# A block of two feed-forward layers around an attention layer: rows of the later feed-forward norms turned by VectorE and DRAM instead of TensorE

## Chip, cores and metric

The kernel runs on one core of one Trainium2 chip. The metric is the device time of one execution in microseconds (us); the time of a run of the kernel before is the median of three, 376.88 us.

## The reference

The input has 16 sequences of 256 rows with 128 features. All is float32; the weights of the feed-forward layer are -1, 0 or 1 with a scale per output column.

```
x = x + 0.5 * ffn(layernorm(x))
x = x + attention(layernorm(x))          # (with a second norm inside, gamma and beta)
x = x + 0.5 * ffn(layernorm(x))

ffn(x):  h = silu(x W1 s1) * (x W2 s2);  h = gelu(h H1 sh1);  h = gelu(h H2 sh2);  return h W3 s3
attention(x):  h = LN(x) gamma + beta;  keys = h Wk + bk;  values = h Wv + bv
               w = exp((keys Wka + bka) / sqrt(128));  w = w / cumsum(w)
               return cumsum(w * keys) * values
```

The hidden width is 512. Both feed-forward layers use the same weights. Cumulative sums run along a sequence.

## The kernel before

The 4096 rows are cut into 8 tiles of 512. Each tile goes through the feed-forward layer, the attention layer and the feed-forward layer again, so there are 16 feed-forward tiles (t = 0 to 15; t from 8 on is the second pass) and 8 attention tiles. Everything stays in SBUF. The residual lies transposed, features on the partitions, in `xt_sb`; matmuls take and give this layout. A norm needs rows on the partitions: for t < 8 they come from `x_sb`, else TensorE turns a tile of `xt_sb` into the bank `y_ps` (stage `u`, four transposes of 128x128, L462).

A norm has these stages. VectorE takes `stats` (four `bn_stats`, L825), `aggr` (a `memset` of one column and four `bn_aggr`, L827 to L832) and `veps` (two small instructions, L839 and L840). GpSimd raises to the power -0.5 and multiplies (`norm`, L362 and L364). ScalarE writes the normalised rows to `z` (stage `z`, four instructions, L726; `zwait` is its wait). TensorE turns `z` into the bank `xt_ps` (stage `t`, `transpose4`, L462). For a feed-forward tile ScalarE copies the bank to `xn_hi`, rounded to fp32r (L764), and VectorE writes the rest to `xn_lo` (L913); for an attention tile ScalarE writes `h_t` with gamma and beta (L767).

The feed-forward layer runs in fp32r with each activation split into a high and a low part, so that two matmuls of 512 columns stand for one product (L449). Stage `p1` gives `gate_ps` and `up_ps` from `xn_hi` and `xn_lo` (four chunks of four matmuls), `p2` and `p3` the hidden layers in `hid_ps` (four chunks of eight each), and `p4` gives `y_ps` (eight). ScalarE does `tanh`, `gelu2`, `gelu3` and the high parts (`high1` to `high3`), VectorE does `gate`, `up`, the low parts (`low1` to `low3`, L877) and the residual (`dt`, L930). The attention has three fp32 products (`att_logits`, `att_keys`, `att_values`; L632, L629, L635), an exponential on ScalarE, which loads its table there and back, and on VectorE two scans, two reciprocals (L940) and some products.

There is no planner at run time. `START`, `SECOND_LAYER`, `FIRST_STEP`, `ORDER` and `LAST_STEP` are lists written out, one per engine and step, and `schedule` issues each engine's stages in that order; semaphores couple the engines. A step i is about one feed-forward tile of PE's time. `AHEAD` says how many tiles a stage runs ahead of the step: `stats`, `z` and `u` two, `t`, `p1`, `tanh`, `gate`, `up` one. The middle repeats a group of three steps with two attention tiles (`a` and `b`) four times. The buffer `z` is single: ScalarE writes the next `z` when TensorE has turned the last one (`s_t`). SyncE (SP) only issues the loads, and at the end seven stores of 256 KB and two halves of the last (L340, L343).

Of the kernel before, what the change touches and what calls it, by code (L numbers as in the profile page):

```python
# [4 lines left out]
P = 128  # L5
# [8 lines left out]
TOK = 512  # L14
# [18 lines left out]
        "hi:w1 hi:w2 zwait z",  # L33
        "t vec:s1 bits:h1.1 bits:h1.3 tanh.0 tanh.1 tanh.2 high1.0 tanh.3 high1.1 zwait z.0 z.1 high1.2 bits:h2.0 "
# [15 lines left out]
FIRST_STEP = {  # L50
# [6 lines left out]
}  # L57
ORDER = {
# [5 lines left out]
    ),  # L64
    "ACT": (
# [24 lines left out]
LAST_STEP = {  # L90
    "PE": "p2.0 p2.1 p2.2 p2.3 p4 p3.0 p3.1 p3.2 last:p4a last:p3.0 last:p3.1 last:p4b last:p4c.0 last:p4c.1",
    "ACT": "gelu2.0 gelu2.1 high2.0 high2.1 gelu2.2 high2.2 gelu2.3 high2.3 gelu3.0 high3.0 gelu3.1 high3.1 "
           "gelu3.2 high3.2 last:gelu.0 last:gelu.1",
    "DVE": "low2.0 low2.1 low2.2 low2.3 low3.0 low3.1 dt low3.2 last:dt.0 last:dt.1",
}

POOL_FIRST = ("norm", 1, 2)

AHEAD = {"stats": 2, "aggr": 2, "veps": 2, "norm": 2, "zwait": 2, "z": 2, "t": 1, "p1": 1, "tanh": 1, "gate": 1,
         "up": 1, "high1": 1, "low1": 1, "u": 2, "p4": -1, "dt": -1}  # L100


def macaron_block(nc, x, xt, w1t, w2t, h1t, h2t, w3t, wkt, wkat, wvt, wkn, vecs, out, seq):
# [8 lines left out]
    GROUP, ATT = 3, 2
    FIRST = 2
    LOOPS = NT // ATT
    assert FIRST + GROUP * LOOPS + 2 == 2 * NT
# [883 lines left out]
```

## Time and profile before

| | |
|---|---|
| median of 3 runs | 376.88 us (376.24 to 377.13) |
| span of the profiled execution, first to last instruction | 374.9 us |
| own time of that execution | not recorded; the median lies 1.98 us above the span |
| TensorE busy | 368.0 us |
| VectorE busy | 321.9 us |
| ScalarE busy | 314.1 us |
| GpSimd busy | 52.6 us |

The profile shows one execution. Busy time is the time in which an engine has an instruction under way; instructions of one engine overlap at their ends, so the distance from one start to the next (the pitch) can be shorter than the duration. TensorE's granted clock is full in every slice of the page. A chain of work is followed back from the last instruction: at each step to what released it, or to the instruction before it on its engine.

### The profile page before, as it was taken

Reading aid. Unit: us, or ns where it says so; the run is one execution under the profiler, and the core shown is the slowest. Engines: PE = TensorE matmul, PEld = TensorE weight load, DVE = VectorE, ACT = ScalarE, POOL = GpSimd, SP = SyncE. Lnnn points to the kernel's source line nnn. Section 1 sums busy time; section 2 is a strip of 40 time slices with the busy share of each in tenths; the row PEclk is TensorE's granted clock in tenths of the full one; section 3 lists DMA queues with packets and bytes.
Section 4 is the critical chain, followed back from the end, with each engine's and each line's share of the span. In section 5 each row is a group of like instructions: output and inputs, shape, how many; then the busy total and the mean of one; then the engine's idle time right before and its main releaser. Section 6 shows DMA issues by size and latency. Waiting matters only on the chain.

```text
span 374.9 us, 5278 instructions
## 1 busy us (share of the span) xinstructions
PE 368.0 (98%) x1662; PEld 291.9 (78%) x1662; DVE 321.9 (86%) x713; ACT 314.1 (84%) x549; POOL 52.6 (14%) x67
## 2 busy tenths in 40 slices
PE   7999999999999999999999999999999999999996
PEld 2678888787787877778788787778877778788885
DVE  5898787999999799999988999989799999976733
ACT  4999699989977999798699979967998998686763
POOL 3531101202101202201021120102101210020000
PEclk9999999999999999999999999999999999999999
DMA  7760000000000000000000000000000000000001
GB/s 246 277 265 1 2 0 0 1 2 1 0 2 0 1 2 2 2 0 1 2 0 1 2 1 28 2 28 1 2 29 0 0 30 1 30 1 28 2 0 58
DMA packets 4494, 9.81 MB, mean 26 GB/s; under 512 B 625, under 2 KB 1905, under 8 KB 4209
## 3 DMA queue, kind: packets, MB, share of 16 engines
q1 hardware_dynamic: 3744, 8.65, 6.3%
q10 hardware_dynamic: 720, 0.80, 0.6%
q8 instruction: 15, 0.25, 0.2%
q14 instruction: 15, 0.11, 0.1%
HBM read 7.35 MB, written 2.10 MB: 25 GB/s over the span
## 4 chain that ended last, share of the span: by engine, by line
PE 95%; DMA 2%; DVE 1%; SPq 1%; issue 0%; ACT 0%; ACTq 0%
PE hid_ps L449 60%; PE gate_ps L449 8%; PE y_ps L449 7%; PE up_ps L449 7%; PE xt_ps L462 3%; DMA x_sb<-x 2%; PE y_ps L462 2%; PE xt_ps L632 2%; PE xt_ps L629 2%; PE xt_ps L635 2%; PE up_ps L507 1%; PE gate_ps L507 1%; DVE gate L855 0%; PE xt_ps L449 0%; DVE xt_sb L924 0%
## 5 line engine op out<-in xcount | busy, mean ns | idle before, releaser
L449 PE MATMUL hid_ps<-act_hi,hi_h 128*128 128x512 f32 x480 | 195.6, 408 | 0.0
L449 PE MATMUL hid_ps<-act_lo,hi_h 128*128 128x512 f32 x480 | 186.8, 389 | 0.0
L877 DVE TENSOR_TENSOR act_lo<-full,act_hi 128x512 fp32r<-128x512 f32 x185 | 122.2, 683 | 26.8 <-ACT act_hi L708 24.3
L701 ACT ACTIVATE full<-hid_ps,vec 128x512 f32<-128x512 f32 x123 | 84.4, 686 | 34.9 <-PE hid_ps L449 31.2
L449 PEld LDWEIGHTS hid_ps<-act_hi,hi_h 128*128 128x128 f32 x480 | 90.1, 188 | 22.4 <-issue 4.1
L449 PEld LDWEIGHTS hid_ps<-act_lo,hi_h 128*128 128x128 f32 x480 | 90.2, 188 | 22.1 <-issue 4.3
L708 ACT ACTIVATE act_hi<-full 128x512 fp32r<-128x512 f32 x127 | 78.5, 630 | 2.3
L362 POOL TENSOR_TENSOR rstd<-veps,half 128x4 f32<-128x4 f32 x24 | 35.2, 1467 | 272.5 <-DVE veps L840 272.5
L855 DVE SCALAR_TENSOR_TENSOR gate<-tanh,gate_ps 128x512 f32<-128x512 f32 x60 | 40.6, 679 | 9.2 <-ACT tanh L684 8.6
L684 ACT ACTIVATE tanh<-gate_ps,s_half 128x512 f32<-128x512 f32 x60 | 40.8, 686 | 8.2 <-PE gate_ps L449 8.2
L867 DVE SCALAR_TENSOR_TENSOR full<-up_ps,s_half,gate 128x512 f32<-128x512 f32 x60 | 44.2, 742 | 0.9
L689 ACT ACTIVATE act_hi<-full 128x512 fp32r<-128x512 f32 x60 | 37.3, 621 | 0.2
L940 DVE RECIPROCAL rcsum<-csum 128x256 f32<-128x256 f32 x16 | 27.9, 1743 | 0.0
L449 PE MATMUL gate_ps<-xn_hi,hi_w 128*128 128x512 f32 x59 | 24.7, 419 | 0.0
L726 ACT ACTIVATE z<-y_ps,nmr,rstd 128x128 f32<-128x128 f32 x64 | 24.0, 460 | 0.8 <-POOL nmr L364 0.8
L449 PE MATMUL y_ps<-act_hi,hi_w 128*128 128x512 f32 x60 | 24.2, 403 | 0.0
L449 PE MATMUL y_ps<-act_lo,hi_w 128*128 128x512 f32 x60 | 23.5, 392 | 0.0
L449 PE MATMUL gate_ps<-xn_lo,hi_w 128*128 128x512 f32 x59 | 23.0, 390 | 0.0
L449 PE MATMUL up_ps<-xn_lo,hi_w 128*128 128x512 f32 x59 | 23.0, 390 | 0.0
L449 PE MATMUL up_ps<-xn_hi,hi_w 128*128 128x512 f32 x59 | 23.0, 390 | 0.0
L825 DVE BATCH_NORM_STATS2 stats<-y_ps 128x6 f32<-128x128 f32 x64 | 14.2, 285 | 0.0
L462 PE MATMUL xt_ps<-ident,z 128*128 128x128 f32 x90 | 13.6, 273 | 0.0
(159 smaller groups left out, 397.8 us busy)
## 6 DMA issues: line engine op xcount, KB each, us to landing
xt_sb<-xt SPq DMA_DIRECT2D x1, 2048.0 KB, 10.9
out<-xt_sb SPq DMA_DIRECT2D x7, 256.0 KB, 2.0
x_sb<-x SPq DMA_DIRECT2D x1, 1536.0 KB, 6.6
raw_h<-h2t SPq DMA_DIRECT2D x4, 256.0 KB, 7.3
raw_h<-h1t SPq DMA_DIRECT2D x2, 256.0 KB, 5.9
raw_w<-w2t ACTq DMA_DIRECT2D x1, 256.0 KB, 4.0
raw_w<-w1t SPq DMA_DIRECT2D x1, 256.0 KB, 3.8
raw_h<-h1t ACTq DMA_DIRECT2D x1, 256.0 KB, 6.7
```

Source lines behind the costliest of these rows:

```text
L362: eng.tensor_tensor(rstd[:, :], veps[:, :], half[:, :], ALU.pow).then_inc(s_pow, 1)
L449: mm = eng.matmul(ps, w, a, start=(first and n == 0), stop=(last and n == len(seq_) - 1))
L462: mm = eng.transpose(dst[:, j * P:(j + 1) * P], src[:, j * P:(j + 1) * P], ident[:, :])
L684: eng.activation(tanh_b[m % 2][:, :], gate_home(T, m)[:, :], ACT.Tanh, scale=s1_half[:, m:m + 1]).then_inc(s_tanh, 1)
L689: eng.activation(act_hi[first_act(T)][:, m, :], full1[m % 2][:, :], ACT.Copy).then_inc(s_hi[1], 1)
L701: eng.activation(full23[m % 2][:, :], home23(n, T, m)[:, :], ACT.Gelu, scale=col("sh1" if n == 2 else "sh2", m)).then_inc(s_gelu[n], 1)
L708: eng.activation(act_hi[n][:, m, :], full23[m % 2][:, :], ACT.Copy).then_inc(s_hi[n], 1)
L726: zz = eng.activation(z[:, j * P:(j + 1) * P], norm_blk(kind, t, j), ACT.Identity, bias=nmr[:, j:j + 1], scale=rstd[:, j:j + 1])
L855: eng.scalar_tensor_tensor(gate_b[m % 2][:, :], tanh_b[m % 2][:, :], 1.0, gate_home(T, m)[:, :], ALU.add, ALU.mult).then_inc(s_gate, 1)
L867: eng.scalar_tensor_tensor(full1[m % 2][:, :], up_home(T, m)[:, :], s12_half[:, m:m + 1], gate_b[m % 2][:, :], ALU.mult, ALU.mult).then_in ...
L877: eng.tensor_tensor(act_lo[a][:, m, :], full[m % 2][:, :], act_hi[a][:, m, :].bitcast(F32), ALU.subtract).then_inc(s_lo[n], 1)
L940: eng.reciprocal(rcsum[:, b], csum[:, b]).then_inc(s_rc, 1)
```

## The change

Three things are changed, and the orders of all engines with them.

First, the rows of the feed-forward norms of tiles 3 to 15 (all but `BY_PE`) are not turned by TensorE. VectorE transposes `z` in blocks of 32x32 into `zt_b` (stage `turn`), SyncE writes that to the DRAM scratch `turns` and, when it has landed, reads it back in four transfers with the blocks in their places (pieces of 32 elements) into `xnt_b`. ScalarE's and VectorE's stage `t` read `xnt_b` from SBUF instead of `xt_ps`. Both buffers are double. The next `z` waits for `s_turn`. The attention's norms and the tiles 0 to 2 are still turned by TensorE.

Second, from norm 3 on the statistics of the halves are pooled on GpSimd (`aggregate`, seven small instructions) instead of `bn_aggr` and `veps` on VectorE. `stats` has two buffers.

Third, the orders are one list of 16 steps for each engine (`STEPS`), SyncE and GpSimd among them. The attention tiles a0 to a7 are spread over steps 1 to 13. `zwait` is part of `z`.

```diff
...
-        "p2.0 a:u t p2.1 p2.2 p1.0 p1.1 p2.3 p1.2 a:t p4 p1.3 a:logits u p3.0 p3.1 a:keys p3.2 p3.3",
...
-        "a:stats low2.0 a:aggr t a:veps low2.1 gate.0 up.0 gate.1 up.1 low2.2 gate.2 low1.0 low2.3 dt up.2 low1.1 "
-        "stats gate.3 aggr up.3 veps a:cumsum low3.0 a:recip.0 low1.2 low3.1 low1.3 low3.2 a:recip.1 low3.3",
...
+STEPS = {
...
+        "a0:norm norm",
...
+        "p2.0 p4 p2.1 u p1.0 p1.1 p2.2 p2.3 p1.2 a4:u a3:values p3.0 p3.1 p1.3 p3.2 p3.3",
...
+        "gelu2.0 t high2.0 tanh.0 tanh.1 gelu2.1 high2.1 z gelu2.2 high2.2 gelu2.3 high2.3 high1.0 gelu3.0 "
+        "tanh.2 high1.1 high3.0 tanh.3 gelu3.1 high3.1 high1.2 9:t high1.3 gelu3.2 a4:z gelu3.3 high3.2",
...
+        "gate.0 5:low3.2 up.0 5:low3.3 a2:weight_keys a2:pool low2.0 a2:values low2.1 a2:dt gate.1 up.1 "
+        "low1.0 dt low2.2 low2.3 stats gate.2 low1.1 gate.3 up.2 up.3 a3:cumsum turn low3.0 a3:recip.0 low3.1 "
+        "low1.2 low1.3 low3.2 low3.3",
+        "a3:recip.1 dt t stats low2.0 a3:weight gate.0 gate.1 a3:weight_keys up.0 up.1 turn low2.1 a4:stats "
+        "low2.2 low2.3 a3:pool low1.0 gate.2 low1.1 up.2 low3.0 gate.3 up.3 9:t low3.1 low1.2 low1.3 "
+        "a3:values a3:dt low3.2",
...
+BY_PE = (0, 1, 2)
+AGGREGATE = 3
...
+        zt_b = [sb(f"zt_{i}", [P, TOK]) for i in range(2)]
+        xnt_b = [sb(f"xnt_{i}", [P, TOK]) for i in range(2)]
+        turns = nc.dram_tensor("turns", [2, P, TOK], F32).ap()
...
+        by_dma = [key for key in norm_of if key[0] == "ffn" and key[1] not in BY_PE]
+        pe_turns = [sum(1 for k, m in norm_of.items() if m <= n and k not in by_dma) for n in range(3 * NT)]
+        dma_turns = [sum(1 for k, m in norm_of.items() if m <= n and k in by_dma) for n in range(3 * NT)]
+        turn_of = {key: k for k, key in enumerate(by_dma)}
+
+        def slot(kind, t):
+            k = turn_of[kind, t]
+            return k % 2, k // 2
...
-            for t in range(NT - 1):
-                eng.wait_ge(s_x1, NT + t + 1)
-                eng.dma_start(out[:, t * TOK:(t + 1) * TOK], xt_tile(t)).then_inc(s_out, 16)
+            def turn(kind, t):
+                i, use = slot(kind, t)
+                eng.wait_ge(s_turn, turn_of[kind, t] + 1)
+                if use > 0:
+                    eng.wait_ge(s_turned[i], 64 * use)
+                eng.dma_start(turns[i], zt_b[i][:, :]).then_inc(s_parked[i], 16)
+                if use > 0:
+                    before, at = by_dma[turn_of[kind, t] - 2]
+                    eng.wait_ge(*((s_xlo, at) if before == "ffn" else (s_ht, at + 1)))
+                eng.wait_ge(s_parked[i], 16 * (use + 1))
+                blocks = turns[i].rearrange("(s c) (j q r) -> q c j s r", c=32, j=SUB, r=32)
+                for b in range(4):
+                    eng.dma_start(xnt_b[i][32 * b:32 * b + 32, :].rearrange("c (j s r) -> c j s r", j=SUB, r=32),
+                                  blocks[b]).then_inc(s_turned[i], 16)
+
+            def emit(stage, chunk, t):
+                if stage in ("turn", "att_turn"):
+                    turn("ffn" if stage == "turn" else "att", t)
+                elif stage == "store":
+                    eng.wait_ge(s_x1, t + 1)
+                    eng.dma_start(out[:, (t - NT) * TOK:(t - NT + 1) * TOK], xt_tile(t)).then_inc(s_out, 16)
+
+            schedule("SP", emit, "rest")
...
+            def aggregate(n):
+                stats, done = stats_b[n % 2], 6 * (n - AGGREGATE)
+                a, b = (1.0 + EPS, EPS * EPS) if n in att_norms else (1.0, EPS)
+                eng.wait_ge(s_bn, SUB * n + SUB)
+                eng.tensor_tensor(pair_diff[:, :], stats[:, :, 1], stats[:, :, 4], ALU.subtract).then_inc(s_agg, 1)
+                eng.tensor_tensor(pair_sum[:, :, :], stats[:, :, 1:3], stats[:, :, 4:6], ALU.add).then_inc(s_agg, 1)
+                eng.wait_ge(s_agg, done + 1)
+                eng.tensor_tensor(diff_sq[:, :], pair_diff[:, :], pair_diff[:, :], ALU.mult).then_inc(s_agg, 1)
+                eng.wait_ge(s_agg, done + 2)
+                eng.tensor_scalar(var_part[:, :], pair_sum[:, :, 1], a / P, b, ALU.mult, ALU.add).then_inc(s_agg, 1)
+                eng.wait_ge(s_agg, done + 3)
+                eng.tensor_scalar(diff_part[:, :], diff_sq[:, :], a / 4.0, None, ALU.mult).then_inc(s_agg, 1)
+                eng.tensor_scalar(neg_mean[:, :], pair_sum[:, :, 0], -0.5, None, ALU.mult).then_inc(s_agg, 1)
+                eng.wait_ge(s_agg, done + 5)
+                eng.tensor_tensor(veps[:, :], var_part[:, :], diff_part[:, :], ALU.add).then_inc(s_ve, 1)
+                eng.wait_ge(s_agg, done + 6)
+
             def norm(n):
-
+                if n >= AGGREGATE:
+                    aggregate(n)
...
+                n = norm_of[kind, t]
+                first = SUB - act_z(n)
+                if not pair:
+                    eng.wait_ge(s_nmr, n + 1)
+                    if n > 0:
+                        eng.wait_ge(s_t, pe_turns[n - 1])
+                    if n > 0 and dma_turns[n - 1]:
+                        eng.wait_ge(s_turn, dma_turns[n - 1])
...
+                elif stage == "t" and t not in BY_PE:
+                    i, use = slot("ffn", t)
+                    eng.wait_ge(s_p1, MC * t)
+                    eng.wait_ge(s_turned[i], 64 * (use + 1))
+                    eng.activation(xn_hi[:, :], xnt_b[i][:, :], ACT.Copy).then_inc(s_xhi, 1)
...
+                if n >= 2:
+                    eng.wait_ge(s_nmr, n - 1)
                 for j in range(SUB):
                     if (n, j) == (0, SUB // 2):
                         eng.wait_ge(s_x0_half, 16)
-                    eng.bn_stats(stats[:, j, :], norm_blk(kind, t, j)).then_inc(s_bn, 1)
+                    eng.bn_stats(stats_b[n % 2][:, j, :], norm_blk(kind, t, j)).then_inc(s_bn, 1)
...
+                elif stage in ("turn", "att_turn"):
+                    kind = "ffn" if stage == "turn" else "att"
+                    i, use = slot(kind, t)
+                    eng.wait_ge(s_za, norm_of[kind, t] + 2)
+                    if use > 0:
+                        eng.wait_ge(s_parked[i], 16 * use)
+                    eng.transpose(zt_b[i][:, :], z[:, :]).then_inc(s_turn, 1)
...
+                elif stage == "t" and t not in BY_PE:
+                    i, _ = slot("ffn", t)
+                    eng.wait_ge(s_xhi, t)
+                    eng.tensor_tensor(xn_lo[:, :], xnt_b[i][:, :], xn_hi[:, :].bitcast(F32),
+                                      ALU.subtract).then_inc(s_xlo, 1)
```

(The longest lists are left out; of `STEPS`, step 7 of PE, ACT and DVE stands.) What the prediction uses of the other steps: in step 6 DVE has `... gate.3 up.2 up.3 a3:cumsum turn low3.0 a3:recip.0 low3.1 low1.2 low1.3 low3.2 low3.3` before step 7's `a3:recip.1 dt t`, and PE `... p1.3 u a3:logits p3.0 p3.1 a3:keys p3.2 p3.3`. For tile 15, step 13 has `... low3.0 turn low1.2 low3.1 ...` on DVE and `... p3.0 p3.1 p3.2 p3.3` on PE, step 14 `gelu2.0 high2.0 gelu2.1 high2.1 gelu2.2 t ...` on ACT (for tile 15) and `p2.0 p2.1 p2.2 p2.3 p4 p1.0 ...` on PE.

## Rows read from the trace of the kernel before

**Rows 1.** The page: span, busy time by engine, and VectorE's busy tenths in 40 slices.

```profile
span 374.9 us, 5278 instructions
...
PE 368.0 (98%) x1662; PEld 291.9 (78%) x1662; DVE 321.9 (86%) x713; ACT 314.1 (84%) x549; POOL 52.6 (14%) x67
...
DVE  5898787999999799999988999989799999976733
```

**Rows 2.** The page: the chain that ended last, shares of the span.

```profile
PE 95%; DMA 2%; DVE 1%; SPq 1%; issue 0%; ACT 0%; ACTq 0%
```

**Rows 3.** Stretches: length, busy time by engine (instructions), clock, DMA share, GB/s.

```profile
26.00:372.00 346.00, 345.65 (x1563) 277.62 (x1562) 300.82 (x648) 294.27 (x509) 41.04 (x44) 1.00 0.02 6
138.00:208.00 70.00, 70.00 (x318) 55.77 (x317) 64.65 (x143) 61.32 (x106) 9.48 (x10) 1.00 0.00 1
```

**Rows 4.** The chain in order of time: start us, length us, what.

```profile
119.31 5.44 PE hid_ps L449 x24
124.75 0.44 PE y_ps L462 x4
125.19 0.44 PE xt_ps L462 x4
...
236.73 7.30 PE hid_ps L449 x32
...
306.61 7.30 PE hid_ps L449 x32
```

**Rows 5.** Groups of instructions: count, busy us, mean ns, idle before.

```profile
L940 DVE RECIPROCAL rcsum<-csum 128x256 f32<-128x256 f32 x16 | 27.9, 1743 | 0.0
...
L462 PE MATMUL xt_ps<-ident,z 128*128 128x128 f32 x90 | 13.6, 273 | 0.0
```

**Rows 6.** Timeline of VectorE: start us, us, line, operation, count.

```profile
144.43 2.43 DVE L877 TENSOR_TENSOR act_lo<-full,act_hi 128x512 fp32r<-128x512 f32 x4
...
149.51 0.89 DVE L825 BATCH_NORM_STATS2 stats<-y_ps 128x6 f32<-128x128 f32 x4
...
164.83 0.18 DVE L832 BATCH_NORM_AGGREGATE mv<-stats 128x2 f32<-128x6 f32 x1
...
165.12 1.24 DVE L935 TENSOR_TENSOR_SCAN csum<-ones,kw 128x256 f32<-128x256 f32 x2
...
189.78 0.16 DVE L839 TENSOR_SCALAR neg_mean<-mv 128x4 f32<-128x4 f32 x1
...
189.92 0.69 DVE L877 TENSOR_TENSOR act_lo<-full,act_hi 128x512 fp32r<-128x512 f32 x1
190.74 0.75 DVE L867 SCALAR_TENSOR_TENSOR full<-up_ps,s_half,gate 128x512 f32<-128x512 f32 x1
```

**Rows 7.** Timeline of GpSimd.

```profile
152.09 2.52 POOL L362 TENSOR_TENSOR rstd<-veps,half 128x4 f32<-128x4 f32 x1 [9.18 <-DVE veps L840]
...
190.09 1.38 POOL L362 TENSOR_TENSOR rstd<-veps,half 128x4 f32<-128x4 f32 x1 [19.88 <-DVE veps L840]
...
198.33 1.01 POOL L362 TENSOR_TENSOR rstd<-veps,half 128x4 f32<-128x4 f32 x1 [6.18 <-DVE veps L840]
199.41 0.20 POOL L364 TENSOR_TENSOR nmr<-neg_mean,rstd 128x4 f32<-128x4 f32 x1
```

**Rows 8.** Timeline of ScalarE; in brackets the idle time before it.

```profile
154.92 1.51 ACT L726 ACTIVATE z<-y_ps,nmr,rstd 128x128 f32<-128x128 f32 x4 [0.38 <-POOL nmr L364]
```

**Rows 9.** Transfers: SyncE's issues, queue 1, and issues by size with us to landing.

```profile
13.79 0.43 SPq L335 DMA_DIRECT2D wk<-wkt  x1
...
14.74 0.65 SPq L335 DMA_DIRECT2D wv<-wvt  x1
...
q1 hardware_dynamic: 3744, 8.65, 6.3%
...
out<-xt_sb SPq DMA_DIRECT2D x7, 256.0 KB, 2.0
...
wk<-wkt SPq DMA_DIRECT2D x1, 64.0 KB, 6.1
```

More of the change, by code:

```diff
@@ L49 @@
 )
-FIRST_STEP = {
[6 rows of a table removed]
-}
-ORDER = {
[5 rows of a table removed]
+STEPS = {
+    "SP": (
+        "",
+        "turn",
+        "turn",
+        "turn",
+        "turn",
+        "turn",
+        "turn",
+        "turn",
+        "turn",
+        "store turn",
+        "store turn",
+        "store turn",
+        "store turn",
+        "store turn",
+        "store",
+        "store",
+    ),
+    "POOL": (
+        "norm",
+        "norm",
+        "a0:norm norm",
+        "a1:norm norm",
+        "norm",
+        "a2:norm norm",
+        "a3:norm norm",
+        "norm",
+        "a4:norm norm",
+        "a5:norm norm",
+        "norm",
+        "a6:norm norm",
+        "a7:norm norm",
+        "norm",
+        "",
+        "",
+    ),
[19 rows of a table added]
     ),
     "ACT": (
[10 rows of a table removed]
[42 rows of a table added]
     ),
     "DVE": (
-        "a:stats low2.0 a:aggr t a:veps low2.1 gate.0 up.0 gate.1 up.1 low2.2 gate.2 low1.0 low2.3 dt up.2 low1.1 "
-        "stats gate.3 aggr up.3 veps a:cumsum low3.0 a:recip.0 low1.2 low3.1 low1.3 low3.2 a:recip.1 low3.3",
-        "b:stats a:weight b:aggr t b:veps a:weight_keys low2.0 a:pool gate.0 a:values gate.1 low2.1 a:dt up.0 up.1 "
[6 rows of a table removed]
-    ),
-}
[L90 to L95, printed above, removed]
[39 rows of a table added]
+    ),
+}
 POOL_FIRST = ("norm", 1, 2)
-AHEAD = {"stats": 2, "aggr": 2, "veps": 2, "norm": 2, "zwait": 2, "z": 2, "t": 1, "p1": 1, "tanh": 1, "gate": 1,
-         "up": 1, "high1": 1, "low1": 1, "u": 2, "p4": -1, "dt": -1}
+BY_PE = (0, 1, 2)
+AGGREGATE = 3
+AHEAD = {"stats": 2, "aggr": 2, "veps": 2, "norm": 2, "z": 2, "t": 1, "p1": 1, "tanh": 1, "gate": 1,
+         "up": 1, "high1": 1, "low1": 1, "u": 2, "turn": 2, "p4": -1, "dt": -1, "store": -1}
 def macaron_block(nc, x, xt, w1t, w2t, h1t, h2t, w3t, wkt, wkat, wvt, wkn, vecs, out, seq):
@@ L111, in macaron_block @@
     assert D == P and TOK % seq == 0
[L112 to L115, printed above, removed]
+    assert all(len(steps) == 2 * NT for steps in STEPS.values())
     with ExitStack() as ctx:
@@ L179, in macaron_block @@
         flag_i = sb("flag_i", [P, 3], I32)
-        stats = sb("stats", [P, SUB, 6])
+        stats_b = [sb(f"stats_{i}", [P, SUB, 6]) for i in range(2)]
         mv = sb("mv", [P, SUB, 2])
+        fence = sb("fence", [P, 1])
+        pair_sum = sb("pair_sum", [P, SUB, 2])
+        pair_diff = sb("pair_diff", [P, SUB])
+        diff_sq = sb("diff_sq", [P, SUB])
+        diff_part = sb("diff_part", [P, SUB])
+        var_part = sb("var_part", [P, SUB])
         veps = sb("veps", [P, SUB])
-        fence = sb("fence", [P, 1])
         primed = sb("primed", [P, 1])
@@ L214, in macaron_block @@
             sem(n) for n in ("s_bn", "s_mv", "s_ve", "s_pow", "s_z", "s_t", "s_u"))
+        s_agg, s_turn = sem("s_agg"), sem("s_turn")
+        s_parked = [sem(f"s_parked_{i}") for i in range(2)]
+        s_turned = [sem(f"s_turned_{i}") for i in range(2)]
         s_nmr, s_za, s_t_first, s_xhi_half, s_xlo_half = (
@@ L314, in macaron_block, with schedule, step @@
         block = ctx.enter_context(nc.Block())
+        def schedule(engine, emit, part):
+            def step(i, order):
+                for stage, chunk, t in items(order, i):
+                    emit(stage, chunk, t)
+            if part == "start":
+                step(-1 if engine == "PE" else -2, START[engine][0])
+            if part == "first":
+                step(-1, START[engine][1])
+            if part == "second":
+                step(0, SECOND_LAYER)
+            if part == "rest":
+                for i, order in enumerate(STEPS[engine]):
+                    step(i, order)
         @block.sync
@@ L389, in _, with emit @@
             hi("w3", 0)
[L390 to L431 removed]
+            def emit(stage, chunk, t):
+                norm(norm_of["ffn" if stage == "norm" else "att", t])
+            schedule("POOL", emit, "rest")
         @block.tensor
@@ L831, in norm_aggr, with norm_veps @@
                 for j in range(SUB):
-                    eng.bn_aggr(mv[:, j, :], stats[:, j, :]).then_inc(s_mv, 1)
-            def norm_veps(n, a, b):
+                    eng.bn_aggr(mv[:, j, :], stats_b[n % 2][:, j, :]).then_inc(s_mv, 1)
+            def norm_veps(n):
                 eng.wait_ge(s_mv, SUB * n + SUB)
@@ L839, in norm_veps @@
                 eng.tensor_scalar(neg_mean[:, :], mv[:, :, 0], -1.0, None, ALU.mult)
-                eng.tensor_scalar(veps[:, :], mv[:, :, 1], a, b, ALU.mult, ALU.add).then_inc(s_ve, 1)
+                eng.tensor_scalar(veps[:, :], mv[:, :, 1], 1.0, EPS, ALU.mult, ALU.add).then_inc(s_ve, 1)
             def first_norm():
```

105 lines of the change are left out of this document (40 added, 65 removed), and 115 rows, old and new, of tables (FIRST_STEP, ORDER, STEPS).

## The prediction, made before the changed kernel was run

> **What bounds the kernel now.** I read the page first. TensorE (PE) is busy for 98% of the span, VectorE (DVE) for 86%, ScalarE (ACT) for 84% and GpSimd (POOL) for 14% [rows 1]. Busy shares are averages, so the chain that ended last comes next: 95% of the span lies on PE [rows 2]. The busy time by stretch shows how complete that is: from 26 to 372 us PE works 345.65 of 346.00 us, and in a steady stretch of 70 us it works 70.00 while DVE works 64.65 (92%) and ACT 61.32 (88%) [rows 3]. The chain in order of time then gives prices. It has no piece of waiting in the steady part: 24 matmuls of 512 columns take 5.44 us, 0.227 each, and a group of four 128-column transposes takes 0.44 us [rows 4]. Two equal places of the pattern of three feed-forward tiles and two attention tiles lie 69.88 us apart [rows 4]. So PE sets the end, an instruction taken from it comes off the span in full, and anything done to DVE, ACT, POOL or the transfers costs nothing until PE has to wait. PE has no waits left that a better order could recover.
>
> **Part 1: what leaves PE.** Of the 16 feed-forward norms, tiles 3 to 15 no longer have `transpose4` into `xt_ps`: 13 groups of four. The attention's eight groups, the `u` groups into `y_ps` and tiles 0 to 2 stay. A group's price is its length in the chain, 0.44 us [rows 4], not four times the 273 ns of one record [rows 5], since the records overlap. 13 x 0.44 = 5.72 us. Nothing is added on PE; all other matmuls are the same in number and shape, only in another order. The profiled span is 374.9 us and the median time 376.88, so 1.98 us lie around the span. The floor is 374.9 - 5.72 + 1.98 = 371.16 us. Only a few tenths could go further, where two transpose groups that used to be apart now stand together.
>
> **Part 2: DVE.** Pitches count here, from start to start. `low` has 0.60 us: four fill 2.43 [rows 6]. Removed for the 21 norms from number 3 on: the four `bn_aggr` with the fence (164.83 to 165.12, 0.29 us) and the pair for `neg_mean` and `veps` (189.78 to 189.92, 0.14) [rows 6], so 21 x 0.43 = 9.0 us. Added: 13 block transposes of 128x512. No row shows one. The nearest from below is `low`, 128x512 through the same engine, 0.60; from above the reciprocal, 1.74 us for 256 columns [rows 5], so 3.5 for 512. I take 0.6, because a transpose is one pass over the data as `low` is, and the reciprocal is the only slow row. 13 x 0.6 = 7.8 us (up to 45). The low half of `t` reads SBUF instead of PSUM: `low` is such a form and costs the same, so nothing. DVE's own account is about even, -1 us, and it keeps its 8% of air beside PE. If the transpose were 3.5 us, that air (5.35 us per 70 us, plus nothing for PE's own gain) would be overdrawn.
>
> **Part 3: POOL, and what it does to DVE.** Each norm now has seven small POOL instructions ahead of the power: two on `stats`, then five that build `var_part`, `diff_part`, `neg_mean` and `veps`. The small multiplication that stands behind the power costs 0.20 us when nothing disturbs it, and the power 1.01 [rows 7]. The same power took 2.52 when it started beside two DVE instructions with two SBUF inputs [rows 7], so POOL's reads wait for DVE's. Undisturbed the seven take 7 x 0.28 = 2.0 us with the 0.08 between two of them, and perhaps 4.6 us when each waits a good part of a `low`. The removed DVE steps were 0.43, so each norm comes 1.5 to 4.2 us later. Before, ACT's `z` came 4.6 us behind the end of `stats` in the tightest kind of place (149.51 plus 0.8 to 154.92) and ACT waited 0.38 us for it [rows 6, 8]. So ACT will wait for `nmr` in several steps. What is queued behind `z` on ACT are the next gelus and tanhs, and behind them PE. ACT has 12% of air, 2.8 us in a tile of 23 us, and the new orders put `stats` early and `z` late in a step, so I price this at 0 to 0.3 us on PE per norm, and take about 1 us in all. POOL itself is idle for 86% of the span; its own throughput doesn't matter.
>
> In the other direction, the DVE `low` that started at 189.92, beside a running power, held the next instruction until 190.74: 0.82 us instead of 0.60 [rows 6]. So one POOL instruction can cost DVE 0 to 0.2 us. 147 new ones (21 x 7) cost DVE 0 to 29 us; I take 0.08 each, 12 us, which raises DVE from 92% to about 97% in the steady part. That is nearly all its air, and it is why I don't forecast the floor.
>
> The rule of the Trainium skill that bears here (page "SBUF — State Buffer", the section on its doors) is that GpSimd and a DVE instruction with two SBUF inputs exclude each other for a whole instruction. By that rule seven instructions of 0.20 us would cost DVE 1.4 us a norm, the top of my interval; the trace has 0.22 us lost beside a power of 1.38 us, so it doesn't bear out a lock for the whole length.
>
> **Part 4: the way through DRAM.** The path is DVE transpose, `s_turn`, SP writes 256 KB to `turns`, waits for the landing, issues four gathers of 64 KB in pieces of 128 bytes, ACT's copy to `xn_hi`, DVE's `xn_lo`, then `p1`. From below: 0.6 for the transpose, 2.0 for the landing of a 256 KB store, four issues of 0.43, and 2.0 for the last landing, 6.3 us; from above: issues of 0.65 and 6.1 us for the landing of a 64 KB load that stands behind others, 11.3 us [rows 9]. The small pieces: queue 1 took 6.3% of 16 engines' span for 3744 packets, 0.10 us each, so 2048 pieces at full packet price are 12.9 us, and at price by bytes (256 KB of 8.65 MB) 0.7 us [rows 9]. I take 8 us in all, near the low ends, since the queues are otherwise empty then; the far end is about 16.
>
> What is there to hide it? I counted PE's work between the point that releases the turn and its reader. Tile 15: the turn stands behind `low3.0` of step 13, and ACT's `t` behind `gelu2.2` of step 14, so six p2 and p3 groups of eight matmuls lie between, 6 x 1.81 = 10.9 us; `p1.0` comes a p2 and a p4 later, 14.5 us. Tile 8: some 8 us to ACT's `t` and 12 us to `p1.0`. By the orders' lists the others lie between 7 and 13 us to ACT's `t` and at 12 us or more to `p1.0`. The eight DVE instructions between turn and `t` agree (tile 8: six `low`, two reciprocals, one `dt`, 7.6 us). So at 8 us the turn is hidden, with under 1 us to spare in the tight tiles. The stores behind SP's waits start later by at most one turn, and only the two halves of the last one are on the end; no turn is queued beside those.
>
> DVE's new `turn` also waits for `z` on ACT, with `low` and `gate` queued behind it. In most steps the orders put it 0 to 2 us behind `z`, so a late norm reaches DVE as well. That is the way by which parts 2 to 4 add up. Sum: 371.2 plus 1.0 to 1.2 for these waits = **372.3 us**.
>
> **The rivals.**
> (a) The norm chain and the `turn` wait bite in every norm but don't overwhelm: 0.3 us of PE for 13 tiles, 4 us: 375.1, up to no change. For it: every slack drawn on at once. Against: PE has no wait now with DVE at 92%.
> (b) The turn through DRAM is late. `p1.0` lies 12 to 14 us behind the turn, of which ACT's and DVE's halves take 1.1; with 12.8 in the middle PE waits for latency + 1.1 - 12.8. The gain of 0.44 a tile is gone at 12.1 us. At 12.3 us it is 0.6 x 13 = 8 us: 379; at 16 us some 56 us more. Against: the stores, the only transfers that run alone, land in 2.0 us [rows 9]. For: no row has pieces of 128 bytes.
> The Trainium skill speaks for this rival (page "VectorE: DVE Perf Modes", the section on the three transpose paths): a plain strided copy used as transpose is 19 times slower than the transposing one, which it gives as 1.309 us for 128x128, an estimate of 25 us; no row here shows it, and this copy keeps runs of 128 bytes.
> (c) DVE becomes the bound. At 0.2 us per POOL instruction the pattern of 69.88 us has 64.65 - 5 x 0.43 + 3 x 0.6 + 35 x 0.2 = 71.3 us of DVE work, 1.4 over the old length in each of four patterns: 376.88 + 6 = 383. From about 0.15 a piece (69.6) the gain is gone; a transpose of over 1.2 us does the same.
> (d) The turns don't leave PE: excluded by the diff.
>
> **How the numbers follow.** Forecast (371 to 374.5, likeliest 372.3): 0.60. (a) 0.18, of which 0.12 ends below 376.1 and 0.06 within 0.2% of 376.88, about what a measurement of this kernel can tell from no change. (b) 0.13 and (c) 0.09, both slower. Range: 370.9 up to 380.5, which takes in (b) at its decision point and leaves out its far end and (c). Faster 0.72, same 0.06, slower 0.22.
>
> **What would show it.** Right: PE without waits, 52 fewer `ident,z` transposes, and the pattern shorter by about 1.3 us; landing of the gathers under 3 us behind their issue; a block transpose near 0.68 us; POOL's seven within 2 to 4.6 us. Wrong: PE waiting on `xn_hi` or `xn_lo` (b), DVE at 98% or more in the steady part with PE waiting for `act_lo` (c), ACT waiting for `nmr` for over 2.8 us a tile (a). A gather or a transpose several times its price would make the prediction wrong.

## The result, and the profile of the changed kernel

The changed kernel is slower: 384.67 us median of five runs (381.64 to 385.73) against 377.02 (376.24 to 377.36) for the kernel before, a ratio of 1.0191 [1.0155, 1.0227]. The forecast was 372.3 us, and the time lies outside the range of 370.9 to 380.5.

The profiled run took 381.64 us and had the full TensorE clock throughout. The page of the kernel after, span, busy times and VectorE's tenths (compare [rows 1]):

```profile
span 379.9 us, 5288 instructions
...
PE 365.7 (96%) x1610; PEld 285.5 (75%) x1610; DVE 321.8 (85%) x579; ACT 311.7 (82%) x549; POOL 93.1 (25%) x214
...
DVE  5997787999999799889898987889899889966842
```

PE has 52 matmuls less. DVE's busy time is that of before, 321.8 us, and no engine is busier than PE. Yet the span is 5.0 us longer. The stretch from 26 to 366 us of the kernel after (columns as in [rows 3]) shows where it went:

```profile
26.00:366.00 340.00, 332.76 (x1457) 262.63 (x1456) 296.38 (x505) 286.42 (x500) 80.67 (x191) 1.00 0.11 26
```

PE stands still for 7.2 us of 340, where it stood still for 0.35 of 346 before. Since records overlap, busy time hides part of a wait. Counted by starts (each matmul's distance to the next, less the usual distance of matmuls of those kinds), the matmuls between 26 and 367 us come 11.7 us late after and 1.4 before, 10.3 us more. That fills the gap between the span and the floor of part 1: 379.9 - 369.2 = 10.7 us. Two places carry over half of it: 3.5 us in a wait that begins at 235 and 2.4 us in one that begins at 308.

Who waited for whom, kernel after (waiting instruction, releaser: us in total, times, longest):

```profile
POOL pair_diff L532 <- DVE stats L992: 217.9, 21, 20.8
...
ACT z L889 <- POOL nmr L552: 14.8, 12, 3.0
PEld hid_ps L601 <- ACT full L857: 10.6, 9, 3.7
...
DVE zt L1075 <- ACT z L889: 7.0, 7, 2.0
PE hid_ps L601 <- ACT full L857: 6.1, 5, 2.9
...
ACT xn_hi L918 <- DMA xnt<-turns: 1.2, 1, 1.2
```

The first line is GpSimd's free time. The others form one chain: `z` waits for GpSimd's `nmr`; VectorE's turn waits for `z`; TensorE waits for a gelu (L857) that is queued behind `z`. The way through DRAM appears once, with 1.2 us. In the kernel before, the same wait of `z` was small:

```profile
ACT z L726 <- POOL nmr L364: 1.4, 3, 0.6
```

The largest stall, in the timeline of the kernel after (start us, length us, engine, line, operation; in brackets the idle time before it and its releaser):

```profile
229.51 0.89 DVE L992 BATCH_NORM_STATS2 stats<-y_ps 128x6 f32<-128x128 f32 x4 [0.40 <-PE y_ps L614]
...
230.47 0.57 POOL L532 TENSOR_TENSOR pair_diff<-stats 128x4 f32<-128x4 f32 x1 [13.20 <-DVE stats L992]
...
230.86 0.69 ACT L941 ACTIVATE kw<-xt_ps,bka_s 128x512 f32<-128x512 f32 x1
...
231.44 0.68 ACT L840 ACTIVATE tanh<-gate_ps,s_half 128x512 f32<-128x512 f32 x1
231.50 1.28 DVE L1044 TENSOR_TENSOR act_lo<-full,act_hi 128x512 fp32r<-128x512 f32 x2
...
231.71 0.56 POOL L539 TENSOR_SCALAR diff_part<-diff_sq 128x4 f32<-128x4 f32 x1
...
233.52 1.28 POOL L550 TENSOR_TENSOR rstd<-veps,half 128x4 f32<-128x4 f32 x1
...
234.88 0.20 POOL L552 TENSOR_TENSOR nmr<-neg_mean,rstd 128x4 f32<-128x4 f32 x1
235.12 1.51 ACT L889 ACTIVATE z<-y_ps,nmr,rstd 128x128 f32<-128x128 f32 x4 [2.99 <-POOL nmr L552]
236.64 1.28 ACT L857 ACT_TABLE_LOAD   x1
236.65 0.71 DVE L1075 STREAM_TRANSPOSE zt<-z 128x512 f32<-128x512 f32 x1 [2.04 <-ACT z L889]
...
237.93 1.26 ACT L857 ACTIVATE full<-hid_ps,vec 128x512 f32<-128x512 f32 x2
...
238.67 0.50 PE L601 MATMUL hid_ps<-act_hi,hi_h 128*128 128x512 f32 x1 [2.91 <-ACT full L857]
```

`stats` ends at 230.40 and `nmr` at 235.08. Between them ScalarE has two instructions, 1.4 us of work, and then stands for 2.99 us. Behind the late `z` (1.51 us) follow the table load back from the exponential (1.28 us) and only then the gelu that TensorE needs. Almost the whole wait, 2.91 of 2.99 us, arrives on TensorE. The step's list reads `a5:logits tanh.3 z gelu3.0`: `z` stands two items behind the point at which `stats` ends. The stall at 308 is built alike: `z` waits 2.50 us for `nmr`, and the table load stands behind it. Of the 21 norms from number 3 on, 11 have their `z` started within 0.05 us of the end of `nmr`; in the kernel before there are 3.

The orders count as well. Take the room of a norm: the time from the end of its `stats` to the end of what ScalarE does just before its `z`. The way is the time from the end of `stats` to the end of `nmr`. Over the 21 norms, from the timelines:

| | way, mean | room, least | norms with a room under 4.0 us |
|---|---|---|---|
| kernel before | 4.99 us | 4.1 us | 0 |
| changed kernel | 4.27 us | 1.7 us | 9 |

So the way is not longer than in the kernel before, where other work of VectorE stands between `stats`, `bn_aggr` and `veps`. What the change took away is the room: its lists put `z` nearer to `stats`.

The new operations, groups and DMA issues of the kernel after (count, busy us, mean ns; for the issues KB each and us to landing), and one turn on SyncE:

```profile
L1075 DVE STREAM_TRANSPOSE zt<-z 128x512 f32<-128x512 f32 x13 | 9.2, 707 | 7.3 <-ACT z L889 7.0
...
L614 PE MATMUL xt_ps<-ident,z 128*128 128x128 f32 x38 | 5.8, 273 | 0.0
```

```profile
turns<-zt SPq DMA_DIRECT2D x13, 256.0 KB, 2.0
xnt<-turns SPq DMA_DIRECT2D x52, 64.0 KB, 2.5
...
q1 hardware_dynamic: 33072, 15.47, 14.3%
```

```profile
106.93 0.33 SPq L493 DMA_DIRECT2D turns<-zt  x1
108.96 2.60 SPq L500 DMA_DIRECT2D xnt<-turns  x4
```

This turn began on DVE at 106.21. The last of the four gathers is issued 1.96 us behind 108.96 and lands 2.8 us later: 7.5 us in all. The 13 turns took 7.2 to 8.3 us.

### The profile page after: what moved, and what is told of

Same layout as the page of the kernel before. It is cut to its first block and busy times, and to the rows that moved or that the text cites. A ratio compares the mean times of both kernels' runs of the same rounds, so it can differ in the third digit from the quotient of the medians.

```text
span 379.9 us, 5288 instructions
## 1 busy us (share of the span) xinstructions
PE 365.7 (96%) x1610; PEld 285.5 (75%) x1610; DVE 321.8 (85%) x579; ACT 311.7 (82%) x549; POOL 93.1 (25%) x214
## 3 DMA queue, kind: packets, MB, share of 16 engines
q1 hardware_dynamic: 33072, 15.47, 14.3%
## 5 line engine op out<-in xcount | busy, mean ns | idle before, releaser
L601 PE MATMUL hid_ps<-act_hi,hi_h 128*128 128x512 f32 x480 | 192.9, 402 | 6.2 <-ACT full L857 6.1
L857 ACT ACTIVATE full<-hid_ps,vec 128x512 f32<-128x512 f32 x123 | 84.3, 689 | 26.4 <-PE hid_ps L601 23.2
L532 POOL TENSOR_TENSOR pair_diff<-stats 128x4 f32<-128x4 f32 x21 | 10.9, 517 | 217.9 <-DVE stats L992 217.9
L550 POOL TENSOR_TENSOR rstd<-veps,half 128x4 f32<-128x4 f32 x24 | 28.3, 1181 | 11.8 <-DVE veps L1007 9.1
L601 PE MATMUL gate_ps<-xn_hi,hi_w 128*128 128x512 f32 x59 | 26.1, 443 | 0.3 <-ACT full L857 0.3
```

The lines of the kernel that those rows point to most:

```text
L550: eng.tensor_tensor(rstd[:, :], veps[:, :], half[:, :], ALU.pow).then_inc(s_pow, 1)
L601: mm = eng.matmul(ps, w, a, start=(first and n == 0), stop=(last and n == len(seq_) - 1))
L857: eng.activation(full23[m % 2][:, :], home23(n, T, m)[:, :], ACT.Gelu, scale=col("sh1" if n == 2 else "sh2", m)).then_inc(s_gelu[n], 1)
```

## The experiments

In the expectations N is the theory that the norm comes late and drags `z` with it (rival a), C the theory that GpSimd's instructions slow VectorE (rival c), T the theory that the turn through DRAM is late (rival b). Each ratio is to runs of the kernel before on the same chip.

**The changed kernel again.** No edit.

> The changed kernel itself, once more, as the measure for the others on this chip. Its five runs lay between 381.6 and 385.7 us, with granted clocks from 1.000 down to 0.989. Theory N (the norm's chain: z is ordered so close behind stats that ScalarE waits for GpSimd's nmr, and TensorE for the gelu behind it) and all rivals expect 382 to 386 us. If a lower clock is part of the loss, its runs must be ordered by it: about 1 us for each 0.3% of clock.

383.11 us, ratio 1.0182 [1.0150, 1.0215], span 379.8 us, the same waits. The four runs had a mean TensorE clock of 1.0, 1.0, 0.996 and 0.989 and took 381.57, 382.31, 383.91 and 384.82 us in that order: the executions with the lower clock are the longer ones. The same holds for the five runs of the result: 381.64 us at 1.0 and 385.73 at 0.989. As an estimate, 0.011 of 384 us is 4.2, near the difference of 4.1. The kernel before never had less than 0.998.

**The pooling back on VectorE,** directly behind each `stats`, everything else as changed.

```diff
-AGGREGATE = 3
+AGGREGATE = 99
...
                     eng.bn_stats(stats_b[n % 2][:, j, :], norm_blk(kind, t, j)).then_inc(s_bn, 1)
+                if n >= 3:
+                    norm_aggr(n)
+                    norm_veps(n)
```

> The changed kernel with one part undone: bn_aggr and veps of all norms on VectorE again, directly behind each stats, so GpSimd has only the power and the product. Theory N: from the end of stats to nmr 3.0 us instead of 4.3, ScalarE waits 12 times for nmr as before but about 1.2 us less each, PE regains 2 to 5 us: 379 to 382. Rival C (GpSimd's small instructions hold up VectorE): its 150 instructions are gone, all is regained, 372 to 374. Rival T (the way through DRAM): no difference, 383 to 385.

376.35 us, 0.9988 [0.9978, 0.9997]: 6.8 us of the loss are gone, more than N and less than C had given. The way from `stats` to `nmr` is 2.4 us in the mean instead of 4.3. Waits and the stretch, kernel with the pooling on VectorE:

```profile
ACT z L889 <- POOL nmr L552: 2.1, 3, 0.9
...
DVE zt L1079 <- ACT z L889: 1.1, 2, 0.8
```

```profile
26.00:366.00 340.00, 338.14 (x1482) 267.18 (x1481) 309.06 (x655) 290.55 (x504) 32.81 (x44) 1.00 0.11 26
```

14.8 us of `z`'s waits have become 2.1, though VectorE is busier by 12.7 us (309.06 against 296.38). The lists are those of the change, and so is the room (1.7 us at least); only the way is shorter. Both N and C allow a gain here, so this run alone doesn't tell them apart.

**The pooling on GpSimd alone,** in the kernel before with its own orders: the seven instructions and the second `stats` buffer are added, `bn_aggr` and `veps` fall away from norm 3 on.

```diff
+AGGREGATE = 3
...
             def norm(n):
+                if n >= AGGREGATE:
+                    aggregate(n)
...
             def norm_aggr(n):
-
+                if n >= AGGREGATE:
+                    return
```

> The kernel before with one part of the change alone: from norm 3 on the statistics are pooled on GpSimd in seven instructions, the orders of the engines stay, z has its old distance from stats. Theory N: PE never waits, since z stands far enough behind stats there: within 1 us of the kernel before, 376.5 to 378. Rival C: 147 instructions take up to 0.2 us each from VectorE, which has 8% of air: 379 to 384.

376.72 us, 1.0001 [0.9992, 1.0011]: no change. The stretch in the kernel before and in this one, and VectorE beside GpSimd in the timeline of this kernel:

```profile
26.00:366.00 340.00, 340.00 (x1527) 272.83 (x1527) 298.05 (x643) 291.27 (x504) 41.04 (x44) 1.00 0.02 6
...
26.00:366.00 340.00, 340.00 (x1527) 272.85 (x1526) 290.39 (x496) 291.14 (x504) 74.31 (x191) 1.00 0.02 6
```

```profile
162.32 0.68 DVE L907 TENSOR_TENSOR act_lo<-full,act_hi 128x512 fp32r<-128x512 f32 x1
162.92 0.68 DVE L885 SCALAR_TENSOR_TENSOR gate<-tanh,gate_ps 128x512 f32<-128x512 f32 x1
163.51 0.69 DVE L907 TENSOR_TENSOR act_lo<-full,act_hi 128x512 fp32r<-128x512 f32 x1
164.12 0.75 DVE L897 SCALAR_TENSOR_TENSOR full<-up_ps,s_half,gate 128x512 f32<-128x512 f32 x1
```

```profile
162.49 0.58 POOL L370 TENSOR_TENSOR pair_diff<-stats 128x4 f32<-128x4 f32 x1 [7.45 <-DVE stats L853]
163.02 0.20 POOL L371 TENSOR_TENSOR pair_sum<-stats 128x8 f32<-128x8 f32 x1
...
163.74 0.55 POOL L377 TENSOR_SCALAR diff_part<-diff_sq 128x4 f32<-128x4 f32 x1
```

VectorE keeps its pitch of 0.60 us beside them (162.32, 162.92, 163.51, 164.12). It is GpSimd that waits: an instruction of 0.20 us takes 0.55. So C falls. The same seven instructions, with a mean way of 3.9 us from `stats` to `nmr` (4.3 in the changed kernel), cost nothing where the lists leave a room of 4.1 us or more.

**The turn without DRAM.** ScalarE and VectorE read `zt_b` itself; SyncE's transfers are gone. This leaves out that the blocks of 32x32 are put in their places.

```diff
-                    eng.wait_ge(s_turned[i], 64 * (use + 1))
-                    eng.activation(xn_hi[:, :], xnt_b[i][:, :], ACT.Copy).then_inc(s_xhi, 1)
+                    eng.wait_ge(s_turn, turn_of["ffn", t] + 1)
+                    eng.activation(xn_hi[:, :], zt_b[i][:, :], ACT.Copy).then_inc(s_xhi, 1)
```

> The changed kernel without the way through DRAM: ScalarE and VectorE read the block-transposed tile itself, SyncE issues no turn. The blocks aren't put in their places, so this leaves out part of the computation. Theory N: nothing waits for that way but once for 1.2 us, so at most 1 us less: 382 to 385. Rival T (its latency, or its 26000 small packets beside the other traffic, slow the engines): 372 to 375.

383.94 us, 1.0198 [1.0179, 1.0218], the time of the changed kernel with all its waits (`z` for `nmr` 14.5 us, 12 times). T falls: 65 transfers and 7.2 to 8.3 us of latency a tile cost nothing measurable in these orders. This profile also shows the clock, in four stretches around the largest stall:

```profile
225.00:235.50 10.50, 10.50 (x50) 8.34 (x49) 8.12 (x16) 7.25 (x11) 3.96 (x8) 1.00 0.07 26
235.50:240.40 4.90, 1.99 (x7) 1.02 (x6) 1.28 (x2) 4.49 (x9) 0.27 (x2) 1.00 0.00 0
240.40:243.80 3.40, 3.40 (x10) 2.64 (x9) 3.26 (x6) 2.98 (x7) 0.00 (x0) 0.50 0.00 0
243.80:260.00 16.20, 16.20 (x74) 13.03 (x74) 13.61 (x22) 11.47 (x23) 2.52 (x9) 1.00 0.05 18
```

TensorE waits for 2.9 us ahead of 239.4, works again, and from 240.4 on it has a granted clock of 0.50 (1.2 instead of 2.4 GHz) for 3.4 us. The first twelve matmuls behind the wait take 4.45 us from start to start (239.44 to 243.89); the same twelve take 2.86 us in the changed kernel at full clock (238.67 to 241.53). So the lowered clock costs 1.6 us. The span is 381.8 us, 1.9 more than that of the changed kernel.

**Fewer instructions on GpSimd.** Three pooling instructions instead of seven; the term from the difference of the half means is left out of the variance.

```diff
-                eng.tensor_tensor(pair_diff[:, :], stats[:, :, 1], stats[:, :, 4], ALU.subtract).then_inc(s_agg, 1)
...
-                eng.tensor_tensor(veps[:, :], var_part[:, :], diff_part[:, :], ALU.add).then_inc(s_ve, 1)
+                eng.tensor_scalar(veps[:, :], pair_sum[:, :, 1], a / P, b, ALU.mult, ALU.add).then_inc(s_ve, 1)
```

> The changed kernel with three instead of seven pooling instructions on GpSimd (the sum of the halves, neg_mean, veps); the term of the difference of the two half means is left out of the variance, so this leaves out part of the computation. All orders as in the changed kernel. Theory N (the delay from stats to nmr is what costs): 4.3 us becomes 2.7 to 3.2, between the changed kernel (4.3 us, 383) and the run with VectorE's bn_aggr (2.5 us, 376.4): 377 to 380. A rival for that run's gain (that bn_aggr is issued on VectorE directly behind stats, so the other engines' waits fall otherwise): no gain, 382 to 384.

374.74 us, 0.9945 [0.9930, 0.9960], below what was expected. With the orders of the change and all its turns, a way shorter by 1.1 us (3.15 instead of 4.27 in the mean) gives back 8.4 us. ScalarE's waits for `nmr` fall from 14.8 us to 5.3, none over 1.5. This is the plainest evidence for N, and the effect isn't proportional: a quarter of the latency carries most of the loss.

**Moving `z` alone,** then `z` with the turns and the attention's `t`. All instructions are those of the change. In the first, 14 of ScalarE's `z` items are moved by one to seven places, most of them later (in step 11: tile 13's, three places); in the second also 9 of 13 `turn` items on VectorE, four `a:t` on TensorE and some `a:t` on ScalarE. The edit of the first, in step 11:

```diff
-        "... tanh.2 tanh.3 z a6:keys gelu3.0 high3.0 high1.1 ..."
+        "... 12:tanh.2 12:tanh.3 a6:keys 11:gelu3.0 11:high3.0 13:z 12:high1.1 ..."
```

> The changed kernel with its seven GpSimd instructions and its turns through DRAM; only ScalarE's z of 14 norms stands elsewhere in ScalarE's list, mostly one to three instructions later (that of a0 seven), no other list is touched. Theory N (z comes too close behind stats for the longer chain on GpSimd): ScalarE's waits for nmr fall from 14 us to under 8, PE's lost time from 10 us to 5 or 7: 378 to 380.5 us. A rival by which the loss lies in the number of instructions or in the DRAM way, not in their places: 383 as the changed kernel.

> As the run with z alone, and with z also what hangs on it moved by a few places: VectorE's turn (9 of 13), the attention's t on TensorE (4) and on ScalarE. Nothing is added or left out. Theory N: PE's lost time falls to 3 to 5 us, no stall of 2 us or more is left and the clock stays full in each run: 374 to 377.5 us. The rival: 383.

381.43 us, 1.0119 [1.0103, 1.0136], and 378.54 us, 1.0043 [1.0026, 1.0060]: both better than the changed kernel, both about 1 us worse than expected. Waits of the first:

```profile
DVE zt L1024 <- ACT z L838: 9.6, 9, 2.4
ACT z L838 <- POOL nmr L501: 5.4, 6, 2.8
...
PE y_ps L550 <- ACT z L838: 2.5, 1, 2.5
```

ScalarE's waits fall from 14.8 to 5.4 us, but more than ScalarE's own list hangs on a late `z`. VectorE's turn, which kept its place, now waits for 9.6 us instead of 7.0. And `z` reads the bank `y_ps`, which `p4` overwrites: once TensorE waits 2.5 us for that. A late norm can't be repaired at one point.

**All lists rewritten.** Four kernels have new positions for most of the items of the PE, ACT and DVE lists (in `order_pool` 129, 289 and 328 items). Two of them, `order_pool` and `order_pool2`, keep every operation of the change; the other two have the pooling on VectorE. The positions are worked out from the durations in the traces so that each wait has a stated distance. `order_pool`: seven on GpSimd, 7 us allowed from turn to `t`. `order_dve`: pooling on VectorE, likewise. `order_pool2`: seven on GpSimd, 4.5 us from `stats` to `z` and 8.5 us from turn to `t`. `order_dve2`: pooling on VectorE, 8.5 us. A line of ScalarE's list, change and `order_pool2`:

```diff
-        "a5:keys gelu2.0 t tanh.0 high2.0 gelu2.1 tanh.1 high2.1 z gelu2.2 gelu2.3 high2.2 ..."
+        "10:gelu2.0 10:high2.0 11:t 10:gelu2.1 10:high2.1 a5:keys 11:tanh.0 11:tanh.1 10:gelu2.2 10:gelu2.3 12:z ..."
```

> The changed kernel's instructions on every engine, all of them, with pooling on GpSimd and turns through DRAM, in orders that leave 4.5 us between stats and z and 8 us between turn and t wherever they can: many items of TensorE's, ScalarE's and VectorE's lists stand a few places elsewhere, the norms in the same sequence. Theory N: nothing of the loss is in the instructions, so PE's lost time falls from 10 us to 1 to 3 and the time is 372 to 375.5. If a part of the loss is in the instructions (contention, small packets), it stays above 377.

> As the run with bn_aggr and veps on VectorE behind stats (376.4 us, PE's lost time 4.3 us), with orders of TensorE, ScalarE and VectorE that leave room for its shorter chain. Theory N: PE's lost time falls to 1 to 2 us: 371.5 to 374 us, below the kernel before and at most 1 us off the run with pooling on GpSimd and new orders. If VectorE's 9 us more of work count, it comes out slower than that run by 2 us or more.

> As the first run with new orders and pooling on GpSimd (376.2 us), in which ScalarE waited 11.4 us in all for the gathers, since its orders left only 7 us between turn and t; here they leave 8.5 us or more, and 4.5 us between stats and z. Every instruction of the changed kernel is there. Theory N together with the turn's measured length (7.3 to 8 us): ScalarE's wait for the gathers under 2 us, PE's lost time 1 to 2.5 us, 371.5 to 374 us. If the instructions themselves cost something, it stays at 376.

> bn_aggr and veps on VectorE as in the earlier run with new orders (374.4 us), now with 8.5 us between turn and t. ScalarE waited 5.7 us for the gathers there. Theory N with the turn's length: 371.8 to 374 us. If VectorE's load (9 us more than with pooling on GpSimd) is the limit, it stays at 374.4.

| | us | ratio to before | `stats` to `nmr`, mean | `z` for `nmr` | `t` for the gathers |
|---|---|---|---|---|---|
| changed kernel, again | 383.11 | 1.0182 [1.0150, 1.0215] | 4.27 us | 13.9 us, 12x | 1.4 us, 1x |
| order_pool | 376.23 | 0.9991 [0.9977, 1.0006] | 4.63 | 1.9, 3x | 11.4, 8x |
| order_pool2 | 374.72 | 0.9942 [0.9930, 0.9955] | 4.27 | 1.0, 2x | 5.0, 3x |
| order_dve | 374.44 | 0.9939 [0.9925, 0.9953] | 2.59 | 1.4, 2x | 5.7, 5x |
| order_dve2 | 376.69 | 0.9996 [0.9987, 1.0006] | 2.60 | 2.0, 3x | 0.5, 1x |

Waits of `order_pool` and of `order_pool2`, and the stretch of the latter:

```profile
ACT xn_hi L867 <- DMA xnt<-turns: 11.4, 8, 3.1
```

```profile
ACT xn_hi L867 <- DMA xnt<-turns: 5.0, 3, 2.0
...
ACT z L838 <- POOL nmr L501: 1.0, 2, 0.6
```

```profile
26.00:366.00 340.00, 339.62 (x1493) 268.55 (x1492) 300.77 (x509) 291.61 (x508) 81.93 (x191) 1.00 0.11 26
```

`order_pool2` is the decisive run: the same instructions as the change, the same 4.27 us from `stats` to `nmr`, and 8.4 us less time. The least room is 4.3 us instead of 1.7, and only 2 of its 21 `z` start within 0.05 us of `nmr`, not 11. So the latency of the pooling is harmless if the lists leave room for it. `order_pool` shows the price of too short a distance at the other place: with 7 us allowed for the turn, ScalarE waits eight times for the gathers. `order_pool2` and `order_dve` beat the kernel before by 0.6%. All four are slower than expected: `order_pool` and `order_pool2` end 0.7 us above the upper end of their ranges, `order_dve` 0.4 and `order_dve2` 2.7, and none reaches the floor of 371.2 us. The waits of `order_pool2` for the gathers were to fall under 2 us and are 5.0: in three tiles ScalarE is free for `t` 5.7 to 6.1 us behind the start of the turn, not 8.5. For `order_dve2` the expectation had a second case, that it stays at 374.4 if VectorE's load is the limit; its 376.69 fits neither case. `order_dve2` waits less for gathers than `order_dve` and is 2.2 us slower all the same; its waits are many small ones between gelus and low parts, and I can't name one cause.

**A mixture.** `bn_aggr` on VectorE, `neg_mean` and `veps` on GpSimd, with lists of their own.

```diff
-AGGREGATE = 3
+AGGREGATE = 99
...
-                if n >= AGGREGATE:
-                    aggregate(n)
+                if n >= 3:
+                    a, b = (1.0 + EPS, EPS * EPS) if n in att_norms else (1.0, EPS)
+                    eng.wait_ge(s_mv, SUB * n + SUB)
+                    eng.tensor_scalar(veps[:, :], mv[:, :, 1], a, b, ALU.mult, ALU.add).then_inc(s_ve, 1)
+                    eng.wait_ge(s_nmr, n)
+                    eng.tensor_scalar(neg_mean[:, :], mv[:, :, 0], -1.0, None, ALU.mult).then_inc(s_agg, 1)
...
+                if n >= 3:
+                    norm_aggr(n)
```

> bn_aggr on VectorE behind stats (0.3 us of pitch), but veps and neg_mean on GpSimd, two instructions instead of seven; orders that leave 8.5 us between turn and t and 3.5 us between stats and z. Theory N: stats to nmr 2.8 us, PE's lost time 1 to 2 us, 371.5 to 373.5 us, the fastest or as fast as the run with all pooling on GpSimd.

376.95 us, 1.0008 [0.9999, 1.0016], over 3 us worse than expected. Its way is 3.25 us in the mean, but it has a `z` waiting for 2.0 us, and TensorE loses 2.1 us in a stall that ends at 236.6 and 1.5 us in one that ends at 307.1. One tight place is enough; the mean says little.

## Why the prediction was wrong

**Part 1 was right.** 38 `ident,z` transposes are left instead of 90, and the matmuls keep their pitch. The account of the loss closes on that basis: 369.2 us of floor and 10.3 of later starts give 379.5, against a span of 379.9.

**Part 2 was right.** The block transpose takes 0.71 us, and the next instruction starts 0.64 us after it (236.65 to 237.29); 0.6 was taken, 3.5 feared. VectorE's busy time is unchanged.

**Part 3, second half, was wrong but cost nothing.** I charged VectorE 12 us for contention with GpSimd. The kernel before with the seven instructions has 290.39 us of VectorE work in 340 instead of 298.05, less by what `bn_aggr` and `veps` took; it keeps the pitch of 0.60 and the old time. The row behind my charge was misread. In the 0.82 us from 189.92 to 190.74 VectorE works 0.69 and is idle for 0.13: its list has `low1.1 up.3` there, and `up.3` waits for `low1.1`, since it overwrites the buffer that `low1.1` reads. The kernel before has this four times, and with the seven instructions added the same four places have 0.82 again. Beside the longest power, 152.09 to 154.61 [rows 7], VectorE lost nothing:

```profile
151.92 0.68 DVE L947 TENSOR_TENSOR wgt_keys<-wgt,keys 128x512 f32<-128x512 f32 x1
152.52 0.68 DVE L877 TENSOR_TENSOR act_lo<-full,act_hi 128x512 fp32r<-128x512 f32 x1
153.12 1.27 DVE L951 TENSOR_TENSOR_SCAN pooled<-ones,wgt_keys 128x256 f32<-128x256 f32 x2
```

The pitches are 0.60 us. So the trace of before already spoke against this charge, and rival (c) fell with it. The rule I had weighed there, from the Trainium skill (page "SBUF — State Buffer", section "SBUF: two separate sides"), has either side blocked, whichever comes second. The traces show one side alone: GpSimd stretched (0.20 to 0.55 us), VectorE at its pitch of 0.60.

**Part 3, first half, is the step that failed.** The chain of seven instructions was sized right: they take 2.5 us busy plus gaps, and with the same lists the way from `stats` to `nmr` is 4.27 us in the mean with them and 2.42 with the pooling on VectorE directly behind `stats`, 1.85 more, within the 1.5 to 4.2 of the prediction. But the prediction added this to the kernel before as if nothing else moved, and priced it at 0 to 0.3 us a norm from ScalarE's average air of 12% and from the remark that the orders put `stats` early and `z` late. In the tight places the opposite is the case. In the kernel before the way was 4.99 us and the room 4.1 us at least; in the changed kernel the way is 4.27 us and the room goes down to 1.7. For the turn I had counted the work between release and reader in the lists, step by step. For the norm I didn't, and the lists would have shown it: in step 9 two items stand between, 1.4 us of work against a way of over 4. The average air of an engine says nothing on one distance. I also named the right path: `z`, then the gelus behind it, then PE. The term was 1 us; it measured 10.3 at full clock. With the 3.0 us of the lowered clock that makes 371.2 + 10.3 + 3.0 = 384.5 us, against 384.67.

**Rival (a)** had the mechanism, at 4 us; it took an even price for every norm. The price is not even: two norms of 21 carry 5.9 of 10.3 us, where the table load back from the exponential stands behind `z` and in front of the gelu that PE needs. On top comes the lowered clock, in six of nine executions of the changed kernel: from nothing to 4 us, and 3.0 from the profiled run to the median. No row of the steady part of before could show it, since PE never paused there.

**Part 4 was right.** 8 us were taken and 7.2 to 8.3 measured, hidden in all tiles but one; without DRAM the time is the same. Rival (b) fell, yet the point named for it is real: with 7 us allowed in `order_pool`, the wait is there. The Trainium skill's trap of the strided copy (page "VectorE: DVE Perf Modes", section "The three transpose paths") did not spring for pieces of 128 bytes. That page of the Trainium skill gives it for a large stride of the innermost destination, and its 1.309 us is for 128x128 in bf16. This copy writes whole rows from pieces of 32 fp32 elements, and a turn of 128x512 took 7.2 to 8.3 us; my estimate from the figures of the Trainium skill was 25 us for 128x128.

**The waits of `turn` on `z`** had been seen too and priced with the rest; they are 7.0 us, seven times, part of the same chain. Of the signs announced, "ACT waiting for `nmr` for over 2.8 us a tile" was too coarse: the total of 14.8 us is 0.9 a tile, and it was decisive, because single waits reach 3 us.

What stays open: the last 3 us between the best orders and the floor, and why `order_dve2` is behind `order_dve`.

## What to carry to other kernels

When a step of a chain or the order around it changes, take every instruction that waits for it, count the work that its own engine has between the release and the wait in the written order, before and after, and compare that with the latency, place by place; an average share of idle time is no cover. Before a long pitch is taken as the price of contention, look whether the instruction waits there for one of its own engine. Look next at what is queued behind the waiting instruction: here a table load and a gelu turned nearly all of a wait on ScalarE into one on TensorE. A change that removes work from the bounding engine and rewrites its lists needs the lists made for the latencies: the same instructions gave 383 us in one order and 375 in another.

## What the runs showed of the hardware

- A stall of TensorE can cost more than its length. After a wait of 2.9 us its granted clock was 0.50 for 3.4 us in one profile and after one of 2.5 us again in the kernel with only `z` moved (3.4 us from 300.8 on); in the profile of the changed kernel the same stall came without it, and the runs of the changed kernel with a mean clock of 0.989 to 0.996 took 383.52 to 385.73 us, those at 1.0 took 381.57 to 382.31.
- GpSimd's small instructions (4 elements a partition) take 0.20 us and stretch to 0.55 beside VectorE's; beside a row of four `low` one `pair_diff` took 2.39 us in the changed kernel (at 123.06). VectorE's pitch stayed at 0.60.
- The write of 256 KB lands in 2.0 us and gathers of 64 KB in pieces of 128 bytes in 2.5 us; 33072 packets on queue 1 take 14.3% of the engines' time, 8 points more than before for nine times the packets.
